# Cross-attention on one core: the prologue's order, and the place of one of four score tiles in two slots of three

## What is computed

```
x      = layernorm(hidden) * gamma + beta
Q      = split_heads(x @ Wq.T);  K = V = split_heads(context)
scores = Q K^T * 16**-0.5, masked
attn   = softmax(scores) V
out    = hidden + attn @ Wout.T
```

## Time and profile before

| what | value |
|---|---|
| median of 3 runs | 1595.49 us |
| the profiled execution's own time | 1601.01 us |
| its span, first to last instruction | 1599.3 us |
| mean granted clock of TensorE, share of full | 0.967 |
| PE busy | 1432.5 us, 90% |
| DVE busy | 1074.8 us, 67% |
| ACT busy | 753.0 us, 47% |
| POOL busy | 1121.6 us, 70% |
| HBM traffic over the span | 138 GB/s |

### The profile page before, as it was taken

One profiled execution on the slowest core, in us unless ns is written; L12 is line 12 of the kernel. 1 busy time (PEld: TensorE's weight loads), 2 busy tenths in 40 slices (PEclk: granted clock), 3 DMA queues, 4 the chain that ended last, 5 costly groups with the idle time before them and its releaser, 6 DMA issues.

```text
span 1599.3 us, 66930 instructions
## 1 busy us (share of the span) xinstructions
PE 1432.5 (90%) x30464; PEld 1057.1 (66%) x30464; DVE 1074.8 (67%) x3356; ACT 753.0 (47%) x623; POOL 1121.6 (70%) x403
## 2 busy tenths in 40 slices
PE   4878989899999999999998999999998999999886
PEld 3335667667676666767676766767676676767675
DVE  6334767677777677777776767777777777777730
ACT  1123545455555445454554544555554544555553
POOL 1002768787877687877777777787777878777786
PEclk7887999999999899999999989999999999999999
DMA  9101444444444444443435444444444444444320
GB/s 292 54 0 64 154 159 152 148 151 149 147 143 150 151 163 140 154 156 142 160 127 174 153 138 146 152 147 141 151 165 165 152 146 161 150 154 145 132 90 7
DMA packets 39164, 224.94 MB, mean 141 GB/s; under 512 B 4546, under 2 KB 4578, under 8 KB 26882
## 3 DMA queue, kind: packets, MB, share of 16 engines
q1 hardware_dynamic: 38882, 220.68, 40.8%
HBM read 216.90 MB, written 3.77 MB: 138 GB/s over the span
## 4 chain that ended last, share of the span: by engine, by line
PE 71%; ACT 15%; DVE 8%; issue 5%; DMA 1%; SPq 0%; POOL 0%; ACTq 0%; POOLq 0%; DVEq 0%
PE ps L276 21%; PE ps L237 15%; ACT probs L359 14%; PE ps L291 14%; PE ps L305 7%; DVE masked L324 6%; PE ps L268 5%; PE ps L253 4%; PE ps L652 4%; DVE den_inv L348 1%; ACT sums L610 1%; DMA probs<-in_x 1%; DVE stats L540 0%; DVE tile_max L324 0%; ACTq L358 0%
## 5 line engine op out<-in xcount | busy, mean ns | idle before, releaser
L324 DVE CUSTOM_DVE_ANT_0 masked<-ps,mask_tile 112x500 bf16<-112x500 f32 x1536 | 978.3, 672 | 438.8 <-PE ps L237 422.9
L359 ACT ACTIVATE probs<-ps,mask_bias 125x1792 f32<-125x1792 f32 x384 | 673.7, 1754 | 712.3 <-PE ps L276 712.2
L405 POOL TENSOR_TENSOR sums<-probs 125x1792 f32<-125x1792 f32 x128 | 512.1, 4001 | 439.2 <-ACT probs L359 439.2
L237 PE MATMUL ps<-kT,qdb 32*112 32x500 bf16 x1536 | 528.1, 415 | 45.6 <-DVE tile_max L324 31.6
L276 PE MATMUL ps<-qd,kT 32*125 32x112 f32 x12288 | 517.6, 278 | 10.3 <-issue 10.3
L409 POOL TENSOR_TENSOR sums<-sums,probs 125x1792 f32<-125x1792 f32 x128 | 510.3, 3986 | 14.6 <-ACT probs L359 5.3
L276 PEld LDWEIGHTS ps<-qd,kT 32*125 32x125 f32 x12288 | 497.1, 186 | 12.3 <-issue 11.2
L291 PE MATMUL ps<-probs,v 125*32 125x112 f32 x12288 | 382.1, 264 | 4.6 <-issue 4.3
L291 PEld LDWEIGHTS ps<-probs,v 125*32 125x32 f32 x12288 | 301.5, 111 | 81.3 <-issue 64.9
L237 PEld LDWEIGHTS ps<-kT,qdb 32*112 32x112 bf16 x1536 | 162.4, 124 | 183.5 <-DVE tile_max L324 129.1
L268 PE MATMUL ps<-max_rows,ones_row 4*125 4x448 bf16 x1536 | 177.2, 397 | 72.5 <-ACT probs L359 71.3
(11 more groups left out here) (45 smaller groups left out, 246.1 us busy)
## 6 DMA issues: line engine op xcount, KB each, us to landing
kT<-in_kt SPq DMA_DIRECT2D x96, 1000.0 KB, 6.4
v<-in_ctx SPq DMA_DIRECT2D x96, 1000.0 KB
mask_tile<-mask_add SPq DMA_DIRECT2D x32, 328.1 KB, 15.3
x_res<-in_x SPq DMA_DIRECT2D x16, 224.0 KB, 15.8
out<-result SPq DMA_DIRECT2D x16, 224.0 KB, 15.5
probs<-in_x SPq DMA_DIRECT2D x14, 224.0 KB, 8.8
v<-in_wq_t SPq DMA_DIRECT2D x1, 1024.0 KB, 5.6
woutT<-in_wout_t SPq DMA_DIRECT2D x1, 1024.0 KB, 20.6
```

The lines of the kernel that those rows point to most:

```text
L237: nc.tensor.matmul(bank[0:PAIR_Q, 0:KEYS], qdb[rows, b % 2, g, :], keys, start=True, stop=True).then_inc(ring_filled, 1)
L324: nc.vector.tensor_tensor_reduce(out=masked[0:PAIR_Q, t % 2, :], in0=bank[0:PAIR_Q, 0:KEYS], in1=mask_tile[0:PAIR_Q, b % 2, KEYS * c:KEYS ...
L359: nc.scalar.activation(probs[0:LANES, k % PROBS], ps[0:LANES, 0:TILES_R, 0:BANK_Q], ACT.Exp, bias=mask_bias[0:LANES, n:n + 1], scale=SCALE ...
L405: nc.gpsimd.tensor_tensor(total, probs[0:LANES, slot % PROBS], probs[0:LANES, (slot + 1) % PROBS], ALU.add).then_inc(summed, 1)
```

## The change

Prologue: DVE normalises a unit right behind its statistics. ACT's square roots of units 1 to 4 go behind the copies that STD_AFTER names. Unit 1's q fills get no tiles any more; in units 2 to 4 tiles stand between the matmul calls of a q fill, one behind each of the first three and two behind the last, five to a fill. There are 56 tiles, so eleven fills have five and the last fill has one.

Slots: tile 1 stays between the score blocks where k % 3 == 2. In the other slots it stands behind block 3, directly ahead of tile 2. The number of instructions stays as it was.

```diff
--- before.py
+++ after.py
@@ -38,6 +38,8 @@
 UNIT_TILES = [1, 3, 4, 4, 4]
 UNIT_AT = [sum(UNIT_TILES[:u]) for u in range(len(UNIT_TILES))]
 UNITS = len(UNIT_TILES)
+TILES_FROM_UNIT = 2
+STD_AFTER = [("q", 0, 3), ("x", 1, 3), ("q", 1, 0), ("q", 1, 1)]
 LN_TILES = sum(UNIT_TILES)
 FILL_BANKS = [0, 1, 2, 3, 5]
 CONSTS = 10
@@ -567,7 +569,6 @@
                                     ).then_inc(mask_added, 1)
             for u in range(1, UNITS):
                 statistics(u)
-            for u in range(1, UNITS):
                 normalise(u)
             dve.wait_ge(consts, CONSTS)
             for unit in FIRST_TILES[0:MAX_TILES]:
@@ -611,9 +612,8 @@
                                          scale=ln_weights[:, 0, c:c + 1]).then_inc(drained, 1)
                 else:
                     nc.scalar.copy(qT[:, c, PAIR_Q * UNIT_AT[u]:PAIR_Q * UNIT_AT[u] + w], src).then_inc(drained, 1)
-                    if (u, c) == (0, BLOCKS - 1):
-                        for later_unit in range(1, UNITS):
-                            std(later_unit)
+                if (kind, u, c) in STD_AFTER:
+                    std(STD_AFTER.index((kind, u, c)) + 1)
             act.wait_ge(consts, CONSTS)
             spread_rows(act, 0)
             act.wait_ge(mask_added, 2)
@@ -651,11 +651,11 @@
                 for h in range(BLOCKS):
                     mm = nc.tensor.matmul(bank, wqT[:, h, 128 * c:128 * (c + 1)], xT[u % 2][:, h, 0:w],
                                           start=(h == 0), stop=(h == BLOCKS - 1))
-                mm.then_inc(filled, 1)
-                if u > 0:
-                    for unit in FIRST_TILES[tile:tile + 4]:
+                    if h == BLOCKS - 1:
+                        mm.then_inc(filled, 1)
+                    for unit in FIRST_TILES[tile:tile + (h + 5) // 4] if u >= TILES_FROM_UNIT else ():
                         score_tile(pe, unit)
-                    tile += 4
+                        tile += 1
             pe.wait_ge(drained, FILLS)
             pe.wait_ge(consts, CONSTS)
             turn_rows(pe, ("rows", 0))
@@ -667,9 +667,11 @@
                         score_tile(pe, tiles[0])
                     begin_scores(pe, b, k)
                     score_blocks(pe, b, k, (0, 1))
-                    if tiles:
+                    if tiles and k % 3 == 2:
                         score_tile(pe, tiles[1])
                     score_blocks(pe, b, k, (2, 3))
+                    if tiles and k % 3 != 2:
+                        score_tile(pe, tiles[1])
                     if tiles:
                         score_tile(pe, tiles[2])
                     if k >= 5 and k % 3 == 2:
```

## The result

The changed kernel takes 1547.56 us (median of 4 runs, 1533.36 to 1549.89), the one before 1595.42 (4 runs). The ratio is 0.968, 95% interval 0.961 to 0.975: 3.2% faster, and 3 us from the forecast of 1544.5. The profiled execution took 1549.9 us (span 1548.1, before 1599.3).

What follows compares the result with a forecast made beforehand. PE was taken as the bound, held by plain waits and low clock in the prologue and by the exponential in the slots. 1601.0 - 22.7 - 28 = 1550 us profiled; 1595.5 - 51 = 1544.5 us, range 1530 to 1560.

Steps and rivals of the forecast that it cites:

- What bounds: Whole kernel: PE carries 71% of the chain; prologue has plain waits and low clock, slots run begin, scores, exponential, begin.
- Part 1: Prologue, DVE's order: PE starts unit 1 at 18.2 us instead of 27.2, 9.0 us earlier.
- DVE's first tile is no limit: Prologue: DVE could take it at 36.01, read as the mask tile's landing; the first tile comes at about 37.
- Part 2: Prologue, tiles inside fills: 0.54 us a stop, 5.2 a five-tile block; prologue in all -22.7 us, bounds -30 and -11.
- Half clock, +7.5 us: Prologue, units 2 to 4: 7.5 us added for half clock, after 9.7 us before; PE's gaps shorter, x parts stay.
- Part 3: Slots, tile 1 behind the scores: 46 pairs at 0.65 us, 30 us, less 2: -28 us; bounds 0 and -81.
- Begins 3.2 to 3.3 us apart: Sign in slots 1, 2 of even batches and 7, 8 of all: begin-to-begin distance, 3.4 to 3.75 us before.
- No change from slot 2 to 5 and 8 to 11: Sign in the slots: these stay as they were, as projections or DVE's lateness keep them from gaining.
- slots give nothing: Rival, slots: the slack goes to a later wait, only the prologue gains; 1573 us, chance 0.18.
- every moved tile counts: Rival, slots: all moved tiles gain as DVE's lead grows, -81 us; 1492 us, chance 0.08.
- prologue gives nothing: Rival, prologue: a stop between calls of one accumulation costs twice 0.54 us, 24 us more; 1567 us, chance 0.12.
- slower: Rival, slots: the moved tile costs PE its full 0.35 us in all 247 slots, +86; 1659 us, chance 0.05.

Runs made afterwards that it cites:

- e4: The changed kernel with the old order on DVE and ACT (all statistics first, square roots behind unit 0's copies); 1556.9 us, one run.
- e3: The kernel before with only the new DVE and ACT order, unit 4's square root one copy earlier than in the changed kernel; 1590.9 us, ratio 1.000.
- e5: The changed kernel with five tiles behind each whole q fill instead of between its matmul calls; 1573.2 us.
- e6: The changed kernel with tile 1 moved only in slots 6 and 7 of all batches, 0 and 1 of even ones; 1549.4 us, one run.
- e7: The changed kernel with tile 1 moved only in slots 3, 4, 9, 10 of all batches, 0 and 1 of odd ones; 1576.2 us, one run.
- e2: The kernel before with only the slots changed (the moved tile 1), prologue as before; 1579.6 us, ratio 0.992.
- e1: The changed kernel with the slots of before, so only the prologue is changed; 1565.5 us, ratio 0.983.
- e9: The changed kernel with DVE's four reciprocals of a batch moved to where DVE is idle or no tile of PE waits; 1529.7 us, ratio 0.955.
- e10: e1 with the same move of DVE's four reciprocals as e9; 1563.6 us, one run.
- e11: e9 with two buffers for tile_max and the reduction placed behind tile 0 of slot 10; 1521.7 us.
- e12: e11 with tile 1 behind the score blocks in every slot; 1517.7 us, ratio 0.949.

## Why the prediction was right, point by point

- **What bounds** (exponential in the slots, DVE and clock in the prologue): right; ACT's share of the chain fell from 15 to 3%.
- **Part 1, 9 us earlier**: 8.6 (18.63 for 27.20), worth 9.2 by e4. Right as a term. That DVE's first tile is no limit held; that 36.01 was the mask tile's landing was a misreading, as the section on e3 shows, and no term rested on it.
- **Part 2, block of 5.2 us**: 5.21. The stop of 0.54 us, taken from tiles behind whole fills, holds also between calls of one accumulation; that rival (1567) fell. The rule of the Trainium skill (TensorEngine Tiling (Array Packing), Key Properties), that a change of the tiling mode drains the engine, fits this in that a stop costs 0.54 us and a tile by itself 0.21; no run tells a drain from another cause of the difference.
- **Half clock, +7.5 us**: this term was mis-sized; it should have been nothing. The changed kernel spent 9 us at half clock before its first exponential, 7 of them in unit 1, where it was charged already, and the rest behind the last fill. The last copy came at 103.75; the sum without this term is 103.9, with it 111.4. So the prologue gave 30.4 us by that copy and 30.8 by the first exponential, not 22.7: just past the bound of 30, and the copy ahead of the 105 to 120 that were named as a sign. I had carried the x parts over as a cause of half clock. They were as long as before (56.76 to 60.12, with 1.6 us of idleness) and the clock held; e5 points to the pauses between tiles.
- **Part 3, 46 pairs at 0.65 us = 30, less 2**: the medians give 29.3, and e6 and e7 show the division into free and locked slots as it was written. The condition "the next begin waits for the exponential" picks them only together with DVE's lateness, as the section on e6 and e7 says. Begins 3.2 to 3.3 us apart came in all the places named but one: 3.40 into slot 7 of even batches. "No change from slot 2 to 5 and 8 to 11" is close: 10.70 to 10.59 and 11.63 to 11.62 us in even batches, 11.53 to 11.45 and 11.13 to 11.28 in odd.
- **What was not in the sum**: 9 us more of excess over the medians. So the slots gave 21.4 us in the profiled run. The two misses, -8 and +7 us, cancel, and that is luck: the forecast's 1544.5 is nearer to 1547.6 than its terms were, and nearer than the scatter of the runs (1533 to 1550) can tell.
- **Rivals**: "slots give nothing" falls by e2 and e6, "every moved tile counts" by e7, "prologue gives nothing" by e1, "slower" by all of them.

## What to carry to other kernels

Work taken out of a stretch shortens the loop only where the wait at that stretch's end is the one that PE stands in, and only as far as the next limit behind it; look for both slot by slot, and expect slots with extra work on PE or on the engine that empties the banks to give nothing (e7). Such a lock can be opened afterwards, by moving the other engine's side work into its idle places, and that move is then worth more than before (0.86 us a pair of batches in e9, 0.35 in e10). In a phase with pauses, price the clock too: removing them gave more than their own length (e5).

## What the runs showed of the hardware that was not expected

**Holes in PE's stream at fixed places.** PE stops, without waiting for any semaphore, for 0.9 to 2.5 us at a time. Between the first exponential and the last batch there are 4 to 9 such holes of over 0.85 us in a kernel, 99 in the 14 traces, and 74 of them lie in slot 8 of batches 1, 3, 8, 15, 17 and 29, out of 84 possible; e3 has only two of the six. One of them in the changed kernel, between two score matmuls that wait for no semaphore:

```profile
901.49 0.81 PE L278 MATMUL ps<-qd,kT 32*125 32x112 f32 x24
...
904.52 0.49 PE L278 MATMUL ps<-qd,kT 32*125 32x112 f32 x8 [2.22 <-issue]
```

and the windows around it (columns as above; the clock is the third number from the end):

```profile
893.00:902.00 9.00, 8.95 (x219) 6.64 (x222) 6.70 (x21) 4.95 (x3) 8.61 (x5) 1.00 0.74 208
902.00:905.50 3.50, 1.28 (x38) 0.92 (x38) 1.00 (x5) 0.35 (x1) 3.50 (x1) 1.00 0.33 131
905.50:919.00 13.50, 13.10 (x193) 9.69 (x185) 6.65 (x21) 6.00 (x7) 5.77 (x3) 0.50 0.37 140
```

After the hole of 2.2 us in the second window the clock is 0.50, which is the lower level of 1.2 GHz, for 13.5 us.

The traces tell what PE waited for. The profile lists a DMA queue of instructions:

```profile
q8 instruction: 239, 3.92, 1.1%
```

These are 239 packets of 16 KB, one for every 256 or so of the 61,325 matmuls and weight loads. Counted along these, all 99 holes stand at the same place modulo 256. Each of them ends 1.19 to 1.59 us behind the end of a packet of this queue; in the example the packet lasts from 901.87 to 903.18, and PE goes on at 904.52. And that packet always started 6.8 to 10.9 us behind the one before it. Where a kernel has no hole at one of these places, the packet came sooner: the 14th starts 3.7 us behind the 13th in e1 and e10, which run through there, and 7.3 to 8.5 in the 12 kernels that stop. So PE stood because its next block of instructions came late. Why these packets start late, the traces do not show, and no run changed it.

**More half clock with the moved tile.** Between the first exponential and the last batch the four kernels with the slots of before (before, e1, e3, e10) spent 28 to 49 us at half clock and had 17 to 30 us of excess over the medians; the ten with tiles moved had 43 to 79 and 33 to 39. Part of this may be the holes, of which the four have 4 to 8 and the ten have 6 to 9. Eight of the ten (all but e11 and e12) also fall to half clock in slot 10 of some odd batches without a hole, which none of the four does. The long slot 10 (4.8 us to the next exponential in odd batches) is a candidate, but e6 has it nearly as before, 3.99, and falls too. This stays open.
